# Summing A and its transpose for one batch in PSUM, two rounding passes on GpSimd, and new call sequences

## The reference, cut to what matters

```python
sim = einsum(Q, K) / (sqrt(d) * H)                 # 512 x 512 per batch, here hT^T M hT
threshold = top_k(sim, 153)[..., -1:]
A = sigmoid(sim) * (sim >= threshold)
A = (A + swapaxes(A, -1, -2)) * 0.5
x = x + (1 - gamma) * layernorm(x) + gamma * A
# feed-forward on layernorm(x), every product with weights rounded to -1, 0, 1 and rows rounded to 8 bits
x = x + bitlinear(silu(bitlinear(h, w_gate)) * bitlinear(h, w_up), w_down)
```

## Time and profile before

| | |
|---|---|
| median of 3 runs (lowest to highest) | 266.81 us (266.75 to 266.88) |
| the profiled execution: its time, its span | 267.07 us, 265.3 us |
| busy share of the span: PE, DVE, ACT, POOL | 82%, 75%, 70%, 69% |
| granted TensorE clock, mean over the span | 0.921 |

### The profile page before, as it was taken

How to read it: one execution, slowest core, us unless ns; L and a number is a source line. 1 busy time by engine, 2 the same in 40 slices (tenths; PEclk the granted TensorE clock), 3 DMA queues, 4 the chain that set the end, 5 groups by cost and what they waited for, 6 DMA issues and landing times. The chain is left out here.

```text
span 265.3 us, 3675 instructions
## 1 busy us (share of the span) xinstructions
PE 216.9 (82%) x974; PEld 105.6 (40%) x974; DVE 198.1 (75%) x335; ACT 185.4 (70%) x321; POOL 182.2 (69%) x358
## 2 busy tenths in 40 slices
PE   7755022574769999989998998999979999999993
PEld 7311010353326544434443543444444444444443
DVE  0398596879857999879588979989798586666651
ACT  2698798988987999998899499472707337251700
POOL 1177878888899788877878888897596844307300
PEclk9996555579797999999999999999999999999999
DMA  5999999978792033898190004176404250811976
GB/s 158 363 388 387 360 387 254 277 221 153 133 238 91 19 63 60 164 214 121 35 184 0 0 9 93 21 142 138 80 0 79 43 99 0 168 52 29 261 193 232
DMA packets 78887, 39.19 MB, mean 148 GB/s; under 512 B 67728, under 2 KB 70288, under 8 KB 78352
## 3 DMA queue, kind: packets, MB, share of 16 engines
q1 hardware_dynamic: 78864, 38.94, 58.8%
HBM read 17.96 MB, written 4.19 MB: 84 GB/s over the span
## 5 line engine op out<-in xcount | busy, mean ns | idle before, releaser
L426 PE MATMUL GU<-WuT,xqT 128*128 128x512 f16 x256 | 61.5, 384 | 2.9 <-DMA WuT<-S 1.6
L549 ACT ACTIVATE sg<-GU,gsc 128x1024 f32<-128x1024 f32 x32 | 35.5, 1109 | 37.7 <-PE GU L412 35.2
L412 PE MATMUL GU<-WgT,xqT 128*128 128x512 f16 x256 | 61.1, 382 | 0.4 <-DMA xqT<-qx 0.4
L445 PE MATMUL DN<-WdT,S 128*128 128x512 f16 x208 | 47.5, 379 | 2.1 <-DVE X L845 1.1
L776 DVE TENSOR_TENSOR S<-GU,sg 128x1024 f32<-128x1024 f32 x31 | 37.8, 1219 | 15.3 <-PE GU L426 9.8
L1067 POOL TENSOR_SCALAR S<-S,qh 128x2048 f16<-128x2048 f32 x15 | 30.1, 2005 | 20.3 <-DVE qh L839 19.8
L532 ACT ACTIVATE junk_r<-rows,srch 128x512 int8<-128x512 f32 x48 | 34.1, 716 | 7.1 <-POOL srch L968 7.1
L426 PEld LDWEIGHTS GU<-WuT,xqT 128*128 128x128 f16 x256 | 25.0, 99 | 34.7 <-DVE S L776 4.4
L412 PEld LDWEIGHTS GU<-WgT,xqT 128*128 128x128 f16 x256 | 25.0, 99 | 33.3 <-issue 3.7
L781 DVE TENSOR_REDUCE amh<-S 128x1 f32<-128x2048 f32 x15 | 34.2, 2277 | 0.2
L445 PEld LDWEIGHTS DN<-WdT,S 128*128 128x128 f16 x208 | 20.0, 98 | 26.7 <-DMA S<-S 2.0
(11 more groups left out here) (144 smaller groups left out, 356.7 us busy)
## 6 DMA issues: line engine op xcount, KB each, us to landing
S<-in_L_ffn_w_gate SPq DMA_DIRECT2D x4, 1024.0 KB, 9.5
X<-in_x SPq DMA_DIRECT2D x4, 1024.0 KB, 13.6
S<-in_L_ffn_w_up SPq DMA_DIRECT2D x4, 1024.0 KB, 14.4
S<-in_L_ffn_w_down SPq DMA_DIRECT2D x4, 1024.0 KB, 6.0
out<-X SPq DMA_DIRECT2D x15, 256.0 KB, 2.9
C<-in_ctx SPq DMA_DIRECT2D x2, 256.0 KB, 4.3
C<-in_ctx SPq DMA_DIRECT2D x1, 512.0 KB, 13.8
S<-S SPq DMA_TRANSPOSE x17, 4.4
```

Of the source, the lines that this page charges most:

```text
L412: last = nc.tensor.matmul(G[:, c * 512:(c + 1) * 512], xqT[:, t, k, :], WgT[:, 4 * n:4 * n + 4, k, :], start=(k == 0), stop=(k == KD - 1))
L426: last = nc.tensor.matmul(U[:, c * 512:(c + 1) * 512], xqT[:, t, k, :], WuT[:, 4 * n:4 * n + 4, k, :], start=(k == 0), stop=(k == KD - 1))
L445: last = nc.tensor.matmul(down_bank(i)[:, :], hqT(i)[:, k, :], WdT[:, k, :], start=(k == 0), stop=(k == KF - 1))
L549: A(sg[:, u % 2, :], G[:, :], ACT.Silu, scale=gsc[:, b % 2, t:t + 1]).then_inc(silu_done, 1)
```

## The change: what it does

1. Batch 0 no longer has `add_a` and `a_transposes`. Instead PE adds both in one PSUM bank with float32 matmuls: `a_rows(j)` multiplies the identity (stationary) with the block row A[j] (512 columns), and `a_columns(j)` accumulates onto it four 128x128 products of A's blocks with the identity, which are the transposed block. x1 then adds the sum to X. Its `w_ready` for batch 0 is now counted up by `lnx`. Batches 1 to 3 are as before.
2. The first rounding pass of groups 2 and 3 of the gate weights moves from DVE to a new POOL call, `gate_round`, with its own semaphore; DVE waits for it ahead of the second pass.
3. The call lists of all five engines are written anew. The order of the pieces changes in many places; what each piece does does not.

```diff
+        AWAY = (2, 3)
...
-            x_load(0); w_load(1, w_up, 0); w_load(1, w_up, 3); x_load(3); w_load(1, w_up, 1); c_load(1, 2, 4)
...
+            c_load(1, 2, 4); w_load(1, w_up, 0); x_load(0); w_load(1, w_up, 1); w_load(1, w_up, 2)
+            w_load(2, w_down, 1); w_load(1, w_up, 3); w_transpose(0, 1); x_load(2); x_load(1); x_load(3)
...
+            def a_rows(j):
+                pe.wait_ge(a_ready, j + 1)
+                if j == 1:
+                    pe.wait_ge(s_wscale, 2)
+                if j >= 2:
+                    pe.wait_ge(x1_ready, j - 1)
+                nc.tensor.matmul(at_bank(0, j)[:, :], identf[:, :], SIG[:, j, :], start=True, stop=False)
+
+            def a_columns(j):
+                pe.wait_ge(a_ready, NT)
+                for s in range(NT):
+                    last = nc.tensor.matmul(at_bank(0, j)[:, s * P:(s + 1) * P], SIG[:, s, j * P:(j + 1) * P],
+                                            identf[:, :], start=False, stop=s == NT - 1)
+                last.then_inc(aT_psum, 1)
...
-                    if w == 0:
+                    if w == 0 and g in AWAY:
+                        dve.wait_ge(s_wi0, AWAY.index(g) + 1)
+                    elif w == 0:
                         V.tensor_scalar(q.bitcast(I16), STAGE[w][:, g * GROUP:(g + 1) * GROUP],
                                         ws[:, w:w + 1], 1.0, ALU.mult, ALU.min)
                         dve.drain()
...
+            def gate_round(g):
+                pool.wait_ge(s_wscale, 1)
+                G_.tensor_scalar(QUANT[0][:, g, :].bitcast(I16), STAGE[0][:, g * GROUP:(g + 1) * GROUP], ws[:, 0:1], 1.0,
+                                 ALU.mult, ALU.min).then_inc(s_wi0, 1)
```

More of the change, by code:

```diff
@@ L321, in _ @@
[L321 to L325, removed]
@@ L484, in _ @@
[L484 to L488, removed]
@@ L590, in _ @@
[L590 to L604, removed]
@@ new lines, in _ @@
+            w_round(1, 1); tanhs(1, 0); tanhs(1, 1); sims(2, 1); tanhs(1, 2); w_round(1, 2); w_abs(2, 3)
+            w_round(1, 3); tanhs(1, 3); sims(2, 2); silu(0); w_abs(2, 0); w_abs(2, 1); w_abs(2, 2); sims(2, 3)
+            silu(1); w_round(2, 0); counts(2, 0, 0); silu(2); x_squares(1, 0); squares(0); silu(3); x_squares(1, 1)
+            evac_hT(3); x_squares(1, 2); x_squares(1, 3); silu(4); squares(1); w_round(2, 1); evac_GT(3); silu(5)
+            counts(2, 0, 1); counts(2, 1, 0); silu(6); w_round(2, 2); sims(3, 0); silu(7); w_round(2, 3); squares(2)
@@ L910, in _ @@
-            last_absmax(2); last_absmax(0); last_absmax(1); last_scale(); last_round(0); final(12); last_round(1)
-            final(13); final(14); final_last(0); final_last(1)
+            w_quant(0, 1); x_stats(0, 0, 1); sim_stats(1, 0, 1); x_stats(0, 2, 3); rank(0, 0); rank(0, 1); rank(0, 2)
+            w_quant(0, 2); sim_stats(1, 2, 3); rank(0, 3); note_misses(0); threshold(0); general_path(0)
+            masked(0, 0); masked(0, 1); masked(0, 2); masked(0, 3); w_scale(1); x_stats(1, 0, 1); x1(0, 0); x1(0, 1)
@@ new lines, in _ @@
+            x_stats(1, 2, 3); w_quant(0, 3); x_sqmax(0, 0); x1(0, 2); x1(0, 3); w_quant(1, 0); x_sqmax(0, 1)
+            x_sqmax(0, 2); x_floor(0, 0); x_sqmax(0, 3); x_floor(0, 1); x_floor(0, 2); x_floor(0, 3)
+            x_stats(2, 0, 1); x_stats(2, 2, 3); rank(1, 0); rank(1, 1); rank(1, 2); rank(1, 3); w_quant(1, 1)
+            w_quant(1, 2); note_misses(1); threshold(1); general_path(1); w_quant(1, 3); sim_stats(2, 0, 1)
+            masked(1, 0); masked(1, 1); masked(1, 2); masked(1, 3); mul(0); w_scale(2); sim_stats(2, 2, 3); mul(1)
@@ L1089, in _ @@
-            sigmoids(3, 3); add_a(3, 1); add_a(3, 2); add_a(3, 3); h_round(9); h_coef(8, 2); x_pow(3, 0, 1, 2, 3)
-            x_round(3, 0); x_round(3, 1); x_round(3, 2); x_coef(3); h_round(10); h_round(11); h_round(12)
-            x_round(3, 3); h_coef(10, 2); h_round(13); h_round(14); d_coef(3); h_coef(12, 2); h_coef(14, 1)
-            h_coef(15, 1)
+            gammas(); first_threshold(0, 0); first_threshold(0, 1); update(0, 0, 0); update(0, 0, 1); sigmoids(0, 0)
+            update(0, 1, 0); update(0, 1, 1); update(0, 2, 0); update(0, 2, 1); sigmoids(0, 1); sigmoids(0, 2)
@@ new lines, in _ @@
+            update(0, 3, 0); update(0, 3, 1); first_threshold(1, 0); gate_round(2); ln_coef(0); lnx(0, 0); lnx(0, 1)
+            first_threshold(1, 1); update(1, 0, 0); sigmoids(0, 3); update(1, 0, 1); update(1, 1, 0); update(1, 1, 1)
+            lnx(0, 2); gate_round(3); update(1, 2, 0); lnx(0, 3); update(1, 2, 1); ln_coef(1); update(1, 3, 0)
+            lnx(1, 3); update(1, 3, 1); x_pow(0, 2); x_pow(0, 0); x_round(0, 0); x_pow(0, 1); x_round(0, 1)
+            x_round(0, 2); sigmoids(1, 0); lnx(1, 2); x_pow(0, 3); x_coef(0); sigmoids(1, 1); sigmoids(1, 2)
@@ new lines, in _ @@
+            sigmoids(1, 3); lnx(1, 1); first_threshold(2, 0); lnx(1, 0); add_a(1, 0); ln_coef(2); add_a(1, 1)
+            lnx(2, 2); x_round(0, 3); add_a(1, 2); add_a(1, 3); lnx(2, 1); h_round(0); d_coef(0)
+            first_threshold(2, 1); update(2, 0, 0); x_pow(1, 0, 1, 2, 3); x_round(1, 0); x_round(1, 1); h_round(1)
+            update(2, 0, 1); update(2, 1, 0); x_coef(1); h_round(2); h_coef(0, 2); lnx(2, 0); update(2, 1, 1)
+            x_round(1, 2); x_round(1, 3); sigmoids(2, 0); update(2, 2, 0); update(2, 2, 1); h_round(3)
@@ new lines, in _ @@
+            update(2, 3, 0); update(2, 3, 1); first_threshold(3, 0); first_threshold(3, 1); sigmoids(2, 1)
+            h_coef(2, 2); lnx(2, 3); sigmoids(2, 2); update(3, 0, 0); sigmoids(2, 3); update(3, 0, 1); d_coef(1)
+            update(3, 1, 0); update(3, 1, 1); h_round(4); add_a(2, 0); add_a(2, 1); update(3, 2, 0); add_a(2, 2)
+            add_a(2, 3); h_round(5); h_coef(4, 2); x_pow(2, 0, 1, 2, 3); x_round(2, 0); x_coef(2); h_round(6)
+            update(3, 2, 1); x_round(2, 1); update(3, 3, 0); update(3, 3, 1); sigmoids(3, 0); d_coef(2)
```

150 lines of the change are left out of this document (74 added, 76 removed).

## The result

The changed kernel took **271.58 us** (median of 4 runs, 270.19 to 272.70) against 266.85 us for the kernel before on the same chip (4 runs, 266.75 to 267.44): 1.017 times the time, 95% interval 1.011 to 1.023. It is slower; the forecast was 261.5 us, within 257.3 to 266.0. The profiled execution took 272.68 us with a span of 270.9. The four runs fall into two pairs, 270.19 and 270.48 us at a mean granted clock of 0.905 and 272.68 and 272.70 us at 0.899; what parts them was not found.

A forecast was written before the change was run, and what follows sets the result against it. PE was taken as the bound from 85 us on. A lead of -2.9 us into its dense part and -2.4 within it made -5.3 on 267.07, 261.8; less 0.26 for the median, 261.5 us, range 257.3 to 266.0.

The forecast's parts named there:

- Up to batch 0 masked: DVE's list until batch 0's masked ends: less rounding work and waiting, -4.1 us, mark at 43.3 instead of 47.4.
- Into the dense part: From batch 1's masked through silu(0) and gate(1) to up(1): the lead arriving at PE's dense part is -2.9 us.
- The dense part: PE's stretch behind up(1): a lighter DVE list removes part of PE's 6.03 us of waiting, -2.4 us.
- rival D: Early part comes whole and nearly all 6.03 us of PE waiting goes: 257.2 us, up to 259.3; chance 0.17.
- Batch 0's sum in PSUM: Up to batch 0's last x1: add_a waits go, PE's products mostly covered; mark 53.7 against 56.4, -2.7 us.
- Rival A: Before batch 0's x1: x_load(1) lands late and DVE stands still; landing at 52 gives 268.5 us; chance 0.10.
- C: Sum in PSUM: the float32 products are dearer, 4 blocks x 1.4 us less cover, +3: 264.5 us; chance 0.08.
- B: PE idles behind gate(0), new waits from 85 to 200 us lose the lead: 264.5 likely, 266.2 worst; chance 0.22.

The follow-up runs named there:

- e4: The changed kernel with gate_round's minimum on POOL replaced by a multiply by 1.0: 261.14 us, 0.975 of the kernel before.
- e5: e4 with up(0) put back ahead of sims(2, 3) and gate(1) on PE: 259.69 us, 0.973 of the kernel before.
- e10: The new call lists alone, with rounding on DVE and batch 0's add_a and a_transposes as before: 265.26 us, 0.994 of the kernel before.
- e6: The kernel before with batch 0's sum in PSUM alone, old call order, rounding on DVE: 268.99 us, 1.007 of the kernel before.
- e1: The changed kernel with the moved rounding passes back on DVE and no gate_round: 261.18 us, 0.977 of the kernel before.
- e7: e4 with the sum in PSUM undone, batch 0's a_transposes and add_a back: 266.22 us, 0.996 of the kernel before.

## Why the prediction was wrong

Ends or starts of the marks, us:

| mark | before | forecast | changed | e4 |
|---|---|---|---|---|
| batch 0 masked, end | 47.4 | 43.3 | 50.2 | 44.2 |
| last x1 of batch 0, end | 56.4 | 53.7 | 64.2 | 53.7 |
| batch 1 masked, end | 79.3 | 76.0 | 89.2 | 78.4 |
| silu(0), end | 75.3 | 72.9 | 86.5 | 75.8 |
| gate(1), start | 75.4 | 72.9 | 87.5 | 76.7 |
| up(1), end | 84.35 | 80.9 | 96.5 | 85.6 |
| from there to the span's end | 181.0 | | 174.4 | 174.4 |

**The step that failed** is in "Up to batch 0 masked": "gate_round costs POOL about what h_round does for the same 128x2048 shape, 2.005 us, no less than DVE's 1.29, and no more than 4.0, twice the row." It takes 7.16. I took the price by engine and shape and passed over the operation: h_round multiplies twice, gate_round multiplies and takes a minimum, and the trace of before had no such row on POOL of that size. The upper bound, twice the nearest row, was a guess. With it "DVE comes for its result ... at about 34 us, and POOL has it by then" fell: DVE came at 35.5 and waited to 40.28. The same wait came a second time, ahead of the third x1, where I had looked at no wait for POOL. The forecast 261.5 plus the two waits of 10.0 is 271.5; 271.58 was measured, an agreement that rests on the luck told next. The Trainium skill, "GPSIMD Engine Reference", section "Engine selection", calls GpSimd roughly at line rate for operations with one input. Multiply comes near it (1.97 us, where DVE took 1.29 for multiply and minimum); minimum and maximum don't (7.16 and 7.17).

With the operation changed, the total of e4 lies at the forecast (261.14 against 261.5). That is luck: **two other terms were wrong by 4.2 us each, with opposite signs**:

- "Into the dense part", -2.9, was +1.3 in e4 (84.35, the end of its row, to 85.63). Up to the last x1 the marks hold within 0.9 us, the sum's at 53.7 exactly. Then x_round came at 60.20 and the second warming group took 3.78 us at the lower clock (granted 0.50), where I had "2 to 3.4 us by level", so that ACT's copy came at 66.98 instead of 64.3. And I let gate(1) follow silu(0), though sims(2, 3) stands ahead of it and waits for ACT's copy of the block before. e5 mends part of it.
- "The dense part", -2.4, was -6.6. Of this 4.6 are PE's waits, three quarters of the 6.03 us: 82.53 of 84.00 us busy between 116 and 200 in e4, and 82.40 in e10 with the sequences alone, but 77.40 in e6. I had walked the lists and found margins "of 0 to 0.6 us"; that was too pessimistic, and rival D was nearer here. 1.4 more lie behind PE's last product: 2.6 us to the span's end in e4, 4.0 before. SP issued six stores from 256.00 on in the old order, close ahead of the last, and four from 251.34 on in the new one; that the stores make the difference was not tested. I had said that nothing is lost there, since I had read PE's share only up to 252. Of the last 0.6, 0.5 are PE's waits outside that stretch: 0.21 us ahead of it and 0.32 at 252.45 before, 0.05 in e4.

"Batch 0's sum in PSUM", -2.7, has its mechanism right in the new sequences only, and its size is bound to them: 4 to 5 us there, +1.8 in the old ones. Of the -4.1 ahead of it, 3.2 came in e4 (masked ends at 44.2) and 1.8 in e1 (45.6); neither arrives at up(1), which ends at 85.6 and 84.4. Rival A is refuted: in the changed kernel no DVE wait for x's load appears ahead of x_stats(1), in e4 0.30 us and in e7 1.05. C too: 1.05 us a column group. B's mechanism, a lead lost behind gate(0), is what ate the early term; its new waits in the dense part did not come. Two of the rivals' sums start from 267.07, the profiled execution, and give no median: B's end is 265.9, not 266.2, and D's 256.9, not 257.2. D's -3.9 for the early part is worked out nowhere.

## What to carry to other kernels

Price a moved elementwise operation by a row with the same operation on the same engine, not only with the same shape; where the trace has none, the upper bound is open, and the work behind the waiting instruction is the price. A part that shifts work from one engine to another has to be priced in the order it will stand in: the same sum in PSUM cost 1.8 us where four x1 stood in a row and waited for PE, and won 4 to 5 where DVE had other work between them. No run changed that alone, so it is the likely reason and not a shown one. Price the parts of a change separately too: here the new order earned its gain behind up(1), and the rounding none. Look at the tail behind the bound engine's last instruction too.

## What was not expected of the hardware

On GpSimd a float32 tensor_scalar of 128x2048 with multiply and multiply takes 1.97 us, with multiply and minimum 7.16 (int16 or float16 output alike), with multiply and maximum 7.17, 3.6 times as long; on DVE multiply and minimum takes 1.29. In e10 and e1 DVE's first rounding pass took 1.76 and 1.67 us instead of 1.29, while POOL's two lnx beside it took 2.48 us together, against 1.52 in e4; what makes both longer was not isolated.
